# Uneven token parts (36 and 28 tiles instead of 32 and 32) and a later, denser routing of the first part

## The chip, the core and the metric

The kernel runs on one core of a Trainium2 chip, as one launch. The metric is the device time of that launch in microseconds (us). The engines are named as in the profile: PE (TensorE matmul), PEld (TensorE weight load), DVE (VectorE), ACT (ScalarE), POOL (GpSimd) and SP (SyncE, here a queue of DMA issues). Each engine runs its own instructions strictly in order and waits on semaphores.

## The reference

One transformer block on x of shape 4 x 2048 x 256 in f32 (8192 tokens, 64 tiles of 128 tokens). Six modulation vectors per batch come from `silu(c) @ wmod`; two of them gate the two branches.

```python
h = layernorm(x) * (1 + ca) + sa
x = x + ga * attention(h)            # 16 heads of 16, rotary, causal, exact softmax
h = layernorm(x) * (1 + cb) + sb
scores = sigmoid(h @ gate_w); sb_ = scores + gate_bias
# 4 groups of 4 experts: keep the 2 best groups (sum of their 2 best), then the 4 best experts
w = take(scores, tidx) / (sum + 1e-20) * 2.5
y = sum over the 4 chosen experts e of w_e * (silu(h @ w1[e].T) * (h @ w3[e].T)) @ w2[e].T
shared = (silu(h @ ws1.T) * (h @ ws3.T)) @ ws2.T
x = x + gb * (y + shared)
```

## The kernel before

A planner, `plan()`, writes one list of named items with all work in one order. Every engine walks this list and emits the instructions that are its own, so a place in the list is a place in the queue of each engine that has a part in the item.

**Front.** Layer norm, the q, k and v projections and the rotation of all tokens (to about 340 us).

**Attention.** 16 groups `g` (batch `g // 4`, four heads each) of 40 steps `i`. A step is a block of 128 keys against up to 512 queries for four heads: PE makes scores (`sa`, `sb`), ACT exponentiates two pairs (`exp`, L1650, 80 of them in a group), POOL zeroes the upper triangle of the diagonal blocks (`affine_select`, L1803; 16 of the 40 steps, among them the last four), and two steps later PE multiplies with V (`pv`, L1097). In the same steps PE and DVE find the row maxima of the next group (`max`, L1048 on PE, L1463 and L1466 on DVE, 160 per group, four a step; none in group 15).

**Pumps.** Other work is put between the steps by generators that are advanced at a given rate for each step with i >= 2 (`pumped`). `project(b)` is the output projection, the residual, the second layer norm and the router logits of the 16 tiles of batch b (seven items a tile; POOL does five instructions of it, L1816, L1819, L1827, L1833, L1835). Its first half runs from step 19 of group 3, 7, 11 and 15, its second in the next group; for batch 3 the second half lies in the expert stage. `route(p)` is the routing of token part p: a string of some 167 small DVE instructions (sigmoid, ranks by pairwise comparison, counts, slot numbers, L1231 to L1384), each waiting for the one before. `scatter(p)` follows: the slots' tail is zeroed by a DMA of 2 MB from SP (`zero`, L903, after a POOL memset L1839), 16 indirect DMAs for padding (`zpad`, L1844), and then for each tile a load of its rows into one of three buffers (`hs`, L911 on SP, which waits until the scatters of the tile three before have landed) and four indirect DMAs, one for each chosen expert (`scat`, L1852 on POOL).

**Experts.** Jobs of 128 slots, sorted by expert: 4 per tile and 15 of padding, so 143 for each part. Per job: a load of 128 rows (`jload`, L934 on SP), a transpose (`jin`, L1155 on PE), a copy (L1732 on ACT), twelve matmuls (`jgate`, L1170), silu on ACT (L1741), two products on DVE (L1578, L1579), the down projection (`jdown`, L1186) and a store. The load of a job of part p waits for every scatter of that part:

```python
for k in range(3):
    q.wait_ge(s[f"w_s{p}{k}"], s_last[p, k])
sync.dma_start(xq[n % XQ], xg_d[p][128 * i:128 * i + 128, :])
```

Jobs run part 0, then part 1, then 64 jobs of the shared expert. Beside part 0's jobs run the rest of `project(3)`, `route(1)` (5 items a job) and `scatter(1)` (2 a job). Beside part 1's jobs `collect(0)` sums the four expert outputs of each token of part 0: per tile four indirect gathers on POOL (`yg`, L1865), one scaling on ACT (L1701), three multiply-adds (`comb`, L1559), a gate (`gated`) and a residual (`res`) on DVE. Beside the shared jobs runs `collect(1)`; the output of a shared job (`fin`) adds that tile's sum, so the shared job of tile t of part 1 waits for `res` of that tile. At the border from part 1's jobs to the shared ones whatever is left of `collect(0)` is emptied into the list at once (`drain`).

In the attention stage before the change one generator holds both halves of the work, and what is left is emptied behind the last step:

```python
part0 = chain(route(0), scatter(0))
if g >= 8:
    pumps.append([part0, 0.0, 1.05 if g >= 12 else 1.4])
drain(part0)
```

Of the kernel before, what the change touches and what calls it, by code (L numbers as in the profile page):

```python
# [24 lines left out]
FIRST = (0, 32)  # L25
TILES = (32, 32)
# [11 lines left out]
ROUTE_SLOTS = 167  # L38
# [84 lines left out]
def plan():  # L123
# [185 lines left out]
    part0 = chain(route(0), scatter(0))  # L309
# [21 lines left out]
    for n, (g, i) in enumerate(order):  # L331
        if i == 0:
# [5 lines left out]
            if g >= 8:  # L338
                pumps.append([part0, 0.0, 1.05 if g >= 12 else 1.4])
# [43 lines left out]
    drain(part0)  # L383
# [45 lines left out]
    beside = {0: [[chain(proj[3], route(1)), 0.0, 5], [chain(once("route", 1, ROUTE_SLOTS - 1), scatter(1)), 0.0, 2.0]],  # L429
# [35 lines left out]
def program(nc, x, wqk, wv, bqk, bv, wo, ob, gw, gbias, w13, w2, cT, wmod, ropec, ropes, consts, fconst, out):  # L465
# [14 lines left out]
    with ExitStack() as ctx:  # L480
# [19 lines left out]
        tile_e = [tile_es[32 * p:32 * p + 1, :] for p in range(PARTS)]  # L500
# [10 lines left out]
        h2t = A("h2t", [128, 3, 256], F32)  # L511
# [240 lines left out]
        def t_h2(i):  # L752
            return s[f"w_h2{i % 3}"], rows_done["w_h2", i]
# [7 lines left out]
        def _(sync):  # L761
# [11 lines left out]
            for name, *at in o.items:  # L773
# [120 lines left out]
                elif name == "o_h2":  # L894
# [3 lines left out]
                    sync.dma_start(h2_d[128 * i:128 * i + 128, :], h2t[:, i % 3]).then_inc(s[f"w_h2{i % 3}"], 16)  # L898
# [64 lines left out]
        def _(pe):  # L963
# [16 lines left out]
            for name, *at in o.items:  # L980
# [132 lines left out]
                elif name == "o_turn":  # L1113
# [7 lines left out]
                    for f in (0, 1):  # L1121
                        mm = pe.transpose(PB[:, bank, 128 * f:128 * f + 128], h2t[:, i % 3, 128 * f:128 * f + 128], ident[:, :])
# [808 lines left out]
```

## Time and profile before

| | |
|---|---|
| median of 3 runs | 3035.09 us (3031.45 to 3038.47) |
| the profiled execution, its own time | 3028.71 us |
| its span in the trace | 3027.0 us |
| mean granted TensorE clock | 0.978 |
| PE, DVE, ACT, POOL busy | 92%, 76%, 59%, 41% |
| attention groups 1, 2, 5, 6 and 13 | 100.3 us each |
| first transpose of the expert stage, last transpose copy | 2104.28 us, 3006.16 us |

Times inside the trace count from the start of the span. "Busy" is an average over three stages with different limits; what a moved instruction costs has to be read in the group or job where it stands. A group is delimited below by the start of its first exponential (L1650) and that of the next group.

### The profile page before, as it was taken

The numbers are of one execution on the slowest core, as the hardware profiler recorded it, in microseconds if no ns is written. First come the engines' busy times: TensorE is split into PE (matmuls) and PEld (weight loads), VectorE is DVE, ScalarE is ACT, GpSimd is POOL, SyncE is SP. The second block draws the span as 40 slices with busy tenths as digits, with TensorE's granted clock in tenths as the row PEclk, the third lists the DMA queues.
The fourth block names the chain that finished last, engine by engine and source line by source line (L and its number), as shares of the span: only waits on it lengthen the run. The fifth ranks groups of instructions, "written<-read, shape, count | busy, mean of one in ns | idle before, by whom it ended". The sixth has DMA issues, their size and how long they took to land.

```text
span 3027.0 us, 57895 instructions
## 1 busy us (share of the span) xinstructions
PE 2796.0 (92%) x20452; PEld 1454.0 (48%) x20452; DVE 2295.2 (76%) x6063; ACT 1782.2 (59%) x2736; POOL 1252.7 (41%) x1557
## 2 busy tenths in 40 slices
PE   7888799999999999989998999988989999999997
PEld 4433222223332223322223322223888999999996
DVE  7888899998889999899998889932482225666477
ACT  2422476666566766656665567675566666666532
POOL 6766311213521114511113765555306744443276
PEclk9999899999999999999999999999999999999999
DMA  4853323223312332321323425245336756665486
GB/s 165 206 149 103 113 59 67 65 46 75 102 47 47 67 68 62 104 50 31 66 61 90 140 90 133 91 132 161 120 94 216 235 195 185 181 184 172 139 238 192
DMA packets 288762, 358.85 MB, mean 119 GB/s; under 512 B 63484, under 2 KB 241292, under 8 KB 288220
## 3 DMA queue, kind: packets, MB, share of 16 engines
q1 hardware_dynamic: 259740, 281.12, 34.0%
q0 software_dynamic: 26112, 71.34, 7.5%
q8 instruction: 166, 2.72, 0.4%
q10 hardware_dynamic: 2624, 2.69, 0.3%
q14 instruction: 120, 0.98, 0.1%
HBM read 206.25 MB, written 139.21 MB: 114 GB/s over the span
## 4 chain that ended last, share of the span: by engine, by line
PE 45%; DVE 16%; ACT 12%; POOL 7%; issue 7%; DMA 1%; ACTq 0%; SPq 0%; POOLq 0%; DVEq 0%
ACT P L1650 12%; PE PB L1170 11%; DVE mx L1466 7%; PE PB L1097 7%; PE PB L1186 7%; PE PB L1048 5%; PE PB L1067 5%; PE PB L1080 5%; DVE PB L1463 4%; POOL x_slots L1852 4%; PE PB L1155 2%; PE PB L1111 2%; POOL yg L1865 1%; PE PB L1134 1%; POOL x_slots L1844 1%
## 5 line engine op out<-in xcount | busy, mean ns | idle before, releaser
L1650 ACT ACTIVATE P<-PB 128x1024 f32<-128x1024 f32 (+3 forms) x1280 | 1097.6, 894 | 620.2 <-PE PB L1080 615.8
L1466 DVE TENSOR_REDUCE mx<-PB 128x1 f32<-128x512 f32 x1536 | 974.9, 683 | 110.2 <-PE PB L1048 103.3
L1048 PE MATMUL PB<-KO,QO 64*128 64x512 bf16 (+3 forms) x2560 | 769.9, 355 | 76.6 <-DVE mx L1466 36.7
L1097 PE MATMUL PB<-P,V 128*17 128x512 f32 (+3 forms) x5120 | 599.8, 541 | 10.5 <-POOL P L1803 10.4
L1067 PE MATMUL PB<-QO,KO 64*128 64x512 bf16 (+3 forms) x2560 | 543.6, 353 | 62.0 <-ACT P L1650 35.5
L1048 PEld LDWEIGHTS PB<-KO,QO 64*128 64x128 bf16 x2560 | 205.9, 94 | 778.0 <-DVE mx L1466 358.1
L1463 DVE CUSTOM_DVE_ANT_0 PB<-PB,mk 128x128 f32<-128x128 f32 (+3 forms) x1024 | 481.9, 510 | 35.5 <-PE PB L1048 33.2
L1080 PE MATMUL PB<-QO,KO 34*128 34x512 bf16 (+3 forms) x2560 | 502.8, 351 | 0.1
L1803 POOL TENSOR_SCALAR_AFFINE_SELECT P<-P 128x256 f32<-128x256 f32 x512 | 208.0, 412 | 656.9 <-ACT P L1650 651.4
L1170 PE MATMUL PB<-xT,ws 128*128 128x128 f32 x3432 | 433.7, 276 | 5.0 <-ACT xT L1732 5.0
L1170 PEld LDWEIGHTS PB<-xT,ws 128*128 128x128 f32 x3432 | 408.5, 193 | 6.8 <-ACT xT L1732 6.6
L1578 DVE TENSOR_TENSOR haT<-sl,PB 64x128 f32<-64x128 f32 x350 | 101.5, 290 | 401.2 <-ACT sl L1741 399.0
L1865 POOL DMA_INDIRECT yg<-y_slots,sidu x256 | 249.7, 976 | 301.5 <-DVE acc L1559 118.7
L1186 PE MATMUL PB<-W,haT 128*128 x1144 | 298.1, 383 | 11.2 <-DVE haT L1579 8.4
L1741 ACT ACTIVATE sl<-PB 128x256 f32<-128x256 f32 x350 | 134.2, 383 | 259.1 <-PE PB L1170 257.0
L1067 PEld LDWEIGHTS PB<-QO,KO 64*128 64x128 bf16 x2560 | 137.4, 94 | 254.7 <-ACT P L1650 224.2
L1725 ACT ACTIVATE ws<-W 128x768 f32 x286 | 239.4, 837 | 25.1 <-issue 25.1
L1080 PEld LDWEIGHTS PB<-QO,KO 34*128 34x128 bf16 x2560 | 164.5, 94 | 97.9 <-PE PB L1067 31.7
L1186 PEld LDWEIGHTS PB<-W,haT 128*128 128x128 f32 x1144 | 196.1, 191 | 30.3 <-issue 14.6
L1852 POOL DMA_INDIRECT x_slots<-Rsg,sidu x172 | 166.9, 970 | 84.2 <-ACT P L1650 47.4
L1810 POOL TENSOR_TENSOR osb<-osb,rden 128x512 f32<-128x512 f32 x64 | 82.3, 1286 | 242.1 <-DMA rden<-rden_rows 241.9
L1097 PEld LDWEIGHTS PB<-P,V 128*17 128x17 f32 x5120 | 85.3, 95 | 181.6 <-issue 152.8
(174 smaller groups left out, 3104.3 us busy)
## 6 DMA issues: line engine op xcount, KB each, us to landing
xq<-x_slots SPq DMA_DIRECT2D x286, 128.0 KB, 2.8
qk_parts<-pt SPq DMA_DIRECT2D x192, 128.0 KB, 2.4
KO<-qk_parts SPq DMA_DIRECT2D x192, 128.0 KB, 3.9
y_slots<-yo SPq DMA_DIRECT2D x191, 128.0 KB
QO<-qk_parts SPq DMA_DIRECT2D x64, 256.0 KB, 3.4
rden<-rden_rows SPq DMA_DIRECT2D x256, 64.0 KB, 2.1
y_slots<-mx SPq DMA_DIRECT2D x95, 128.0 KB
v_rows<-vst SPq DMA_DIRECT2D x16, 544.0 KB, 3.8
```

The lines of the kernel that those rows point to most:

```text
L1048: mm = pe.matmul(PB[:, bank, 0:n], QO[half, k3, j, 128 * t:128 * t + 128], KO[half, k3, j, 512 * kc:512 * kc + n], start=True, stop=True)
L1067: pe.matmul(PB[:, j, 0:n], KO[rows, k3, j, 128 * kt:128 * kt + 128], QO[rows, k3, j, q0:q0 + n], start=True, stop=False).then_inc(s["sa"], 1)
L1080: pe.matmul(PB[:, j, 0:n], KO[rows, k3, j, 128 * kt:128 * kt + 128], QO[rows, k3, j, q0:q0 + n], start=False, stop=True).then_inc(s["st"], 1)
L1097: mm = pe.matmul(PB[32 * j:32 * j + 17, 7, c0:512], V[:, g % 2, kt, 17 * j:17 * j + 17], P[:, pbuf(g, i, j // 2), j % 2, 0:n], start=kt == ...
L1170: mm = pe.matmul(PB[:, 2 + k, 128 * m:128 * m + 128], w[:, 128 * m:128 * m + 128], xT[:, k, f, :], start=f == 0, stop=f == 1)
L1186: mm = pe.matmul(PB[:, bank, 0:256], haT[:, k, f, :], w, start=f == 0, stop=f == 1)
L1463: dve.tensor_tensor_reduce(PB[:, u.bank[item], 0:n], PB[:, u.bank[item], 0:n], mk[:, 512 - n:512], 1.0, -3.0e38, ALU.add, ALU.max, mx[:, j ...
L1466: dve.tensor_reduce(mx[:, j, t, kc:kc + 1], PB[:, u.bank[item], 0:n], AX.X, ALU.max).then_inc(s["mx"], 1)
L1650: act.activation(P[:, pbuf(g, i, p), :, 0:n], PB[:, 2 * p:2 * p + 2, 0:n], ACT.Exp, scale=0.25).then_inc(s["exp"], 1)
L1725: act.activation(ws[:, k], W13[:, :, bass.ds(of[p, i], 1), :].rearrange("p f o c -> p f (o c)"), ACT.Copy).then_inc(s["ws"], 1)
L1852: pool.indirect_dma_start(xg_d[p][:, :], bass.IndirectOffsetOnAxis(sidu[:, i, j:j + 1], 0), hs[k], None).then_inc(s[f"w_s{p}{k}"], 16)
L1865: pool.indirect_dma_start(yg[:, k, j, :], None, y_d[p][:, :], bass.IndirectOffsetOnAxis(sidu[:, i, j:j + 1], 0)).then_inc(s[f"l_yg{k}"], 16)
```

## The change

Part 0 gets 36 tiles (tokens of batches 0 and 1 and the first four tiles of batch 2) and part 1 gets 28. So there are 159 and 127 jobs, 286 as before. The routing of part 0 needs the logits of four tiles of batch 2 and can't start before group 11. Routing and scatters become two generators: the routing takes 3.2 items a step from group 11 on, and the scatters 1.5 a step as soon as the routing is in the list. Routing tiles are [128, 36 x 16] and [128, 28 x 16]; counts over more than 32 tiles take two matmuls and two copies each. To make room, `h2t` has two buffers instead of three and the sums of tiles 32 to 35 lie in two buffers of the routing (`Rsb`, `Rcm`).

```diff
-FIRST = (0, 32)
-TILES = (32, 32)
+FIRST = (0, 36)
+TILES = (36, 28)
...
-ROUTE_SLOTS = 167
+HALVES = [[(t, min(t + 32, n)) for t in range(0, n, 32)] for n in TILES]
+ROUTE_SLOTS = [165 + 2 * len(x) + 2 * (n > 32) - 2 * (n <= 16) for x, n in zip(HALVES, TILES)]
...
-        while not o.has("o_logits", (FIRST[p] + TILES[p] - 1) // 16, 15):
+        while not o.has("o_logits", (FIRST[p] + TILES[p] - 1) // 16, (FIRST[p] + TILES[p] - 1) % 16):
...
-    part0 = chain(route(0), scatter(0))
+    def once(name, *at):
+        while not o.has(name, *at):
+            yield
+
+    routing = route(0)
+    scattering = chain(once("route", 0, ROUTE_SLOTS[0] - 1), scatter(0))
...
-            if g >= 8:
-                pumps.append([part0, 0.0, 1.05 if g >= 12 else 1.4])
+            if g >= 11:
+                pumps.append([routing, 0.0, 3.2])
+                pumps.append([scattering, 0.0, 1.5])
...
-    drain(part0)
+    drain(routing)
+    drain(scattering)
...
-    jobs += [("s", i // 32, i) for i in range(NT)]
+    jobs += [("s", int(i >= FIRST[1]), i) for i in range(NT)]
...
-        h2t = A("h2t", [128, 3, 256], F32)
+        h2t = A("h2t", [128, HT, 256], F32)
...
+        more = [r[:, :, :].rearrange("p t e -> p (t e)")[:, 256 * k:256 * k + 256] for r in (Rsb, Rcm) for k in (0, 1)]
+        acc = [*(acc_s[:, t, :] for t in range(ACC)), *more]
...
-                    if i >= 3:
-                        q.wait_ge(s["o_turn"], i - 2)
-                        q.wait_ge(*t_h2(i - 3))
+                    if i >= HT:
+                        q.wait_ge(s["o_turn"], i - HT + 1)
+                        q.wait_ge(*t_h2(i - HT))
```

By the list, the routing items of part 0 stood in groups 8 (16), 9 (53), 10 (53) and 11 (45); now 3 stand in the last step of group 11, 121 in group 12 and 47 in group 13. The 16 paddings and 128 scatters stood in groups 11 to 15 (7, 39, 39, 39 and 20), the last in step 21 of group 15; now the 16 paddings and 144 scatters stand in groups 13 (35), 14 (57) and 15 (68).

Three places. First DVE, in a step near the start of group 12, where the maxima of the next group (L1466, L1463; L1476, L1473 in the new file) and the projection of batch 2 stand. Before:

```order
L1508 TENSOR_TENSOR xo<-PB,obB 128x256
L1466 TENSOR_REDUCE mx<-PB 128x1 x4
L1537 COPY L<-PB 128x16
L1463 ISA PB,mx<-PB,mk 128x128
L1463 ISA mx 128x1
...
L1501 RECIPROCAL r_68<-d_67 128x16
L1466 TENSOR_REDUCE mx<-PB 128x1 x2
L1531 TENSOR_SCALAR h2t<-xin,mvf,rsf 128x256
L1514 BN_STATS st6f<-xin 128x6
```

Now, from the same tile's `xo` on:

```order
L1518 TENSOR_TENSOR xo<-PB,obB 128x256
L1258 MEMSET Rrk 128x576
L1239 TENSOR_TENSOR Rsa<-Rsa 128x36x3 x2
L1250 SCALAR_TENSOR_TENSOR Rsa<-Rsa 128x36x3
L1476 TENSOR_REDUCE mx<-PB 128x1 x2
L1511 RECIPROCAL r_68<-d_67 128x16
L1473 ISA PB,mx<-PB,mk 128x384
L1473 ISA mx 128x1
...
L1547 COPY L<-PB 128x16
L1239 TENSOR_TENSOR Rsa<-Rsa 128x36x2 x2
L1250 SCALAR_TENSOR_TENSOR Rsa<-Rsa 128x36x2
L1476 TENSOR_REDUCE mx<-PB 128x1 x4
```

Three or four routing instructions (`Rsa`, `Rrk`) now stand in each step among the maxima, on whose end PE's next maxima wait.

Second POOL, in the last steps of group 15. Before, there are the triangles of the last diagonal blocks (AFFINE_SELECT) and the projection of batch 3:

```order
L1810 TENSOR_TENSOR osb<-osb,rden 128x512
L1803 AFFINE_SELECT P<-P 128x2x128 x4
L1833 TENSOR_TENSOR h2t<-h2t,modB 128x256
L1835 TENSOR_TENSOR h2t<-h2t,modB 128x256
L1827 TENSOR_TENSOR rsf<-vef,mhalf 128x1
L1803 AFFINE_SELECT P<-P 128x2x128 x2
L1816 TENSOR_TENSOR xo<-xo,gaB 128x256
L1819 TENSOR_TENSOR xin<-xo,xin 128x256
```

Now:

```order
L1837 TENSOR_TENSOR rsf<-vef,mhalf 128x1
L1862 DMA x_slots<-Rrk,sidu 22528x256 x2
L1813 AFFINE_SELECT P<-P 128x2x128 x2
L1826 TENSOR_TENSOR xo<-xo,gaB 128x256
L1829 TENSOR_TENSOR xin<-xo,xin 128x256
L1862 DMA x_slots<-Rrk,sidu 22528x256
L1813 AFFINE_SELECT P<-P 128x2x128 x2
L1862 DMA x_slots<-Rrk,sidu 22528x256
L1862 DMA x_slots<-Rsg,sidu 22528x256 x8
L1862 DMA x_slots<-Rrk,sidu 22528x256 x4
```

One or two scatters (L1862) stand between the triangles of each step, and behind the last triangle stand 13 more, ahead of the first `jload` in the list.

Third DVE, at the border from the last job of part 1 to the first shared job. Before, only the job's own work stands there: the copy of part 1's output (L1587), the two products, and then the first sum with `acc` (L1590). `collect(0)` has ended twenty jobs earlier.

```order
L1587 COPY yo<-PB 128x256
L1578 TENSOR_TENSOR haT<-sl,PB 64x128
L1579 TENSOR_TENSOR haT<-sl,PB 128x128
L1590 TENSOR_TENSOR yo<-PB,acc 128x256
```

Now:

```order
L1597 COPY yo<-PB 128x256
L1588 TENSOR_TENSOR haT<-sl,PB 64x128
L1589 TENSOR_TENSOR haT<-sl,PB 128x128
L1569 SCALAR_TENSOR_TENSOR Rsb<-yg,wts,Rsb 128x256 x3
L1575 TENSOR_TENSOR Rsb<-Rsb,GB 128x256
L1581 TENSOR_TENSOR Rsb<-Rsb,xin 128x256
L1569 SCALAR_TENSOR_TENSOR Rcm<-yg,wts,Rcm 128x256 x3
L1575 TENSOR_TENSOR Rcm<-Rcm,GB 128x256
L1581 TENSOR_TENSOR Rcm<-Rcm,xin 128x256
...
L1600 TENSOR_TENSOR yo<-PB,acc 128x256
```

The last three tiles of `collect(0)` (33, 34 and 35; the last two with `Rcm`) stand there in one block of 15 DVE instructions, and the first gathers of `collect(1)` wait for its last multiply-add.

## Rows read from the trace of the kernel before

**Rows 1.** The page, part 1: busy us, share of the span, instructions

```profile
PE 2796.0 (92%) x20452; PEld 1454.0 (48%) x20452; DVE 2295.2 (76%) x6063; ACT 1782.2 (59%) x2736; POOL 1252.7 (41%) x1557
```

**Rows 2.** Windows by group: stretch, length, busy us of each engine, granted clock, DMA

```profile
446.85:547.15 100.30, 95.03 (x802) 26.62 (x802) 91.84 (x235) 69.78 (x84) 17.78 (x37) 1.00 0.26 55
...
759.09:880.89 121.80, 115.73 (x906) 41.73 (x907) 106.67 (x296) 75.00 (x97) 51.18 (x86) 0.99 0.28 76
...
1081.48:1193.12 111.64, 107.86 (x858) 35.60 (x858) 100.85 (x271) 72.02 (x88) 38.36 (x67) 1.00 0.33 76
1193.12:1320.81 127.69, 119.50 (x907) 42.88 (x907) 113.82 (x310) 75.52 (x98) 51.86 (x88) 0.96 0.27 72
1320.81:1431.09 110.28, 102.23 (x802) 29.39 (x802) 107.72 (x288) 69.90 (x84) 19.08 (x37) 0.98 0.23 50
1431.09:1540.46 109.37, 100.92 (x804) 28.34 (x805) 106.65 (x288) 69.90 (x84) 18.77 (x37) 1.00 0.23 50
1540.46:1667.03 126.57, 113.54 (x858) 37.27 (x858) 115.09 (x318) 72.04 (x88) 42.17 (x69) 0.97 0.34 89
1667.03:1796.72 129.69, 118.53 (x906) 42.22 (x907) 109.73 (x296) 75.06 (x97) 93.90 (x130) 0.96 0.41 120
1796.72:1897.02 100.30, 94.86 (x803) 26.58 (x803) 91.91 (x235) 69.74 (x86) 55.79 (x76) 1.00 0.45 119
```

**Rows 3.** Routing instructions on DVE by line: ns min/median/max, shapes

```profile
L1242 DVE SCALAR_TENSOR_TENSOR Rrk<-Rrk,Rcm x15: 211/415/648, 1357.9 to 1445.6; 128x480 f32<-128x480 f32 x1, 128x448 f32<-128x448 f32 x1, 128x416 f32<-128x416 f32 x1, 128x384 f32<-128x384 f32 x1
...
L1270 DVE RECIPROCAL Rsg<-Rrk x2: 3353/3353/3353, 1289.1 to 2182.2; 128x512 f32<-128x512 f32 x2
```

**Rows 4.** Timeline of POOL at the first padding: start, us, instruction, idle before

```profile
1657.15 1.23 POOL L1844 DMA_INDIRECT x_slots<-Rsa,zidu  x1 [7.20 <-DMA x_slots<-Rsa]
```

**Rows 5.** Scatters on POOL in group 13: ns min/median/max

```profile
L1852 POOL DMA_INDIRECT x_slots<-Rsg,sidu x27: 958/976/1008, 1797.4 to 1895.7; - x27
```

**Rows 6.** Windows, group 15 up to its last triangle

```profile
1996.64:2101.98 105.34, 91.64 (x692) 27.98 (x692) 11.55 (x40) 71.76 (x89) 58.83 (x89) 0.97 0.49 151
```

**Rows 7.** The chain that ended last, last padding of part 1: start, us

```profile
2303.71 2.77 DMA x_slots<-Rsa,zidu
```

**Rows 8.** Timeline of all engines where attention ends

```profile
2101.21 0.77 POOL L1803 TENSOR_SCALAR_AFFINE_SELECT P<-P 128x256 f32<-128x256 f32 x2
...
2102.19 1.33 SPq L934 DMA_DIRECT2D xq<-x_slots  x3
...
2104.28 0.69 PE L1155 MATMUL PB<-ident,xq 128*128 128x128 f32 x2 [1.75 <-DMA xq<-x_slots]
...
2109.62 0.44 PE L1155 MATMUL PB<-ident,xq 128*128 128x128 f32 x2 [2.52 <-DMA xq<-x_slots]
```

**Rows 9.** Windows of L1732, one per job: length, ACT busy (x jobs), clock, DMA

```profile
2107.60:2176.40 68.80, 7.63 (x20) 0.97 0.51 149
2176.40:2272.30 95.90, 12.57 (x33) 0.99 0.30 91
...
2855.30:2979.00 123.70, 19.54 (x51) 1.00 0.80 236
```

**Rows 10.** Timeline of the shared jobs: first and last gather of part 1, and the end

```profile
2855.25 0.94 POOL L1865 DMA_INDIRECT yg<-y_slots,sidu  x1 [73.80 <-DMA y_slots<-yo]
...
3006.16 0.36 ACT L1732 ACTIVATE xT<-PB 128x256 f32<-128x256 f32 x1
...
3015.14 1.22 PE L1186 MATMUL PB<-osb,haT 128*128 128x256 f32 x2 [4.05 <-DVE haT L1579]
...
3016.16 1.06 PE L1186 MATMUL PB<-rden,haT 128*128 128x256 f32 x2
...
3018.33 1.11 POOL L1865 DMA_INDIRECT yg<-y_slots,sidu  x1 [0.30 <-issue]
...
3021.78 1.53 DVE L1559 SCALAR_TENSOR_TENSOR acc<-yg,wts,acc 128x256 f32<-128x256 f32 x3 [2.14 <-ACT acc L1701]
...
3024.36 0.42 DVE L1590 TENSOR_TENSOR yo<-PB,acc 128x256 f32<-128x256 f32 x1
```

More of the change, by code:

```diff
@@ L257, in route @@
         o("route0", p)
-        while not o.has("o_logits", (FIRST[p] + TILES[p] - 1) // 16, 15):
+        while not o.has("o_logits", (FIRST[p] + TILES[p] - 1) // 16, (FIRST[p] + TILES[p] - 1) % 16):
             yield
         o("sge", p)
-        for k in range(ROUTE_SLOTS):
-            if k in (81, 82):
-                unit("cnt", p, k - 81)
+        for k in range(ROUTE_SLOTS[p]):
+            if 0 <= k - 81 < 2 * len(HALVES[p]):
+                unit("cnt", p, *divmod(k - 81, len(HALVES[p])))
             o("route", p, k)
@@ L428, in plan @@
             o("jload", n)
-    beside = {0: [[chain(proj[3], route(1)), 0.0, 5], [chain(once("route", 1, ROUTE_SLOTS - 1), scatter(1)), 0.0, 2.0]],
+    beside = {0: [[chain(proj[3], route(1)), 0.0, 5], [chain(once("route", 1, ROUTE_SLOTS[1] - 1), scatter(1)), 0.0, 2.0]],
               NI[0] - XQ: [],
@@ L499, in program @@
         tile_es = A("tile_es", [33, NI[0] + 1], I32)
-        tile_e = [tile_es[32 * p:32 * p + 1, :] for p in range(PARTS)]
+        tile_e = [tile_es[32 * p:32 * p + 1, 0:NI[p] + 1] for p in range(PARTS)]
         gw_s = A("gw_s", [128, 2, 16], F32)
@@ L752, in t_h2 @@
         def t_h2(i):
-            return s[f"w_h2{i % 3}"], rows_done["w_h2", i]
+            return s[f"w_h2{i % HT}"], rows_done["w_h2", i]
         packed = {n: (s[f"w_on{n % OS}"], 64 * (n // OS + 1)) for n in range(64)}
@@ L897, in _ @@
                     q.wait_ge(s["h2"], i + 1)
[L898 removed]
+                    sync.dma_start(h2_d[128 * i:128 * i + 128, :], h2t[:, i % HT]).then_inc(s[f"w_h2{i % HT}"], 16)
                 elif name == "zero":
@@ L1121, in _ @@
                     for f in (0, 1):
-                        mm = pe.transpose(PB[:, bank, 128 * f:128 * f + 128], h2t[:, i % 3, 128 * f:128 * f + 128], ident[:, :])
+                        mm = pe.transpose(PB[:, bank, 128 * f:128 * f + 128], h2t[:, i % HT, 128 * f:128 * f + 128], ident[:, :])
                     mm.then_inc(s["o_turn"], 1)
@@ L1313, in route @@
                 for m, dst in ((0, sa), (1, slot)):
-                    bank = u.bank["cnt", p, m]
-                    q.wait_ge(s["cnt"], o.n("cnt", p, m))
-                    prev()
-                    dve.tensor_copy(dst, PB[:, bank, 0:16 * PT].rearrange("p (t e) -> p t e", e=16)).then_inc(s["cnt_v"], 1)
-                    yield
-                q.wait_ge(s["cnt_v"], 2 * p + 2)
+                    for h, (lo, hi) in enumerate(HALVES[p]):
+                        bank = u.bank["cnt", p, m, h]
+                        q.wait_ge(s["cnt"], o.n("cnt", p, m, h))
+                        prev()
+                        dve.tensor_copy(dst[:, lo:hi, :],
+                                        PB[:, bank, 0:16 * (hi - lo)].rearrange("p (t e) -> p t e", e=16)).then_inc(s["cnt_v"], 1)
+                        yield
+                q.wait_ge(s["cnt_v"], 2 * sum(len(x) for x in HALVES[:p + 1]))
                 tt(slot, slot, sa, ALU.subtract)
```

39 lines of the change are left out of this document (19 added, 20 removed).

## The prediction

> **What bounds the kernel now.** The page gives PE 92% busy and DVE 76% [rows 1], but those are averages over stages, so I read the windows by group first. A plain attention group takes 100.30 us with DVE busy 91.84: DVE has 8.5 us of room. Groups with a projection take 111.64 (first half) and 121.80 (second half), with DVE at 100.85 and 106.67 [rows 2]. Groups 8 to 11 carry the routing of part 0, and the reader is to see two things in them [rows 2]: how much DVE's busy time grew over the like group without routing, and how much the group's length grew. Group 8: +7.15 busy, +5.9 length (over 121.80). Group 9: +15.9, +10.0 (over 100.30). Group 10: +14.8, +9.1. Group 11: +14.2, +14.9 (over 111.64). The routing is thus 52.1 us of DVE, and about two thirds of it shows as time: groups 9 and 10 leave DVE only 2.6 and 2.7 us idle, so there DVE is the bound, and PE waits for maxima. Group 11's surplus is larger than its neighbours' ratio would give. The timeline shows POOL stand still for 7.20 us in it, for the DMA that zeroes the slots' tail, with triangles queued behind it [rows 4]; I put 5.6 us of the 14.9 on that, 9.3 on routing. Group 12, with scatters and projection together, takes 129.69, 7.9 more than group 4 of the same make; group 13, with 39 scatters and no projection, takes exactly the plain 100.30 [rows 2]. So POOL's scatters cost nothing alone, and something beside a projection.
>
> Then the experts. Where nothing disturbs, 51 jobs take 123.70 us, 2.425 a job. The first 20 (beside the projection) take 3.44 each and the next 33 (beside the routing of part 1) 2.91 each [rows 9]. The end is not PE's: the last transpose copy is at 3006.16, yet the span ends at 3027.0. POOL issues 128 gathers from 2855.25 to 3018.33, one in 1.284 us without a pause, and the last sums and the last output hang on them [rows 10].
>
> **The change, term by term** (change of time in us, against the profiled execution's own 3028.71, which is 6.4 below the median 3035.09).
>
> *Routing leaves groups 8 to 11.* -5.9, -10.0, -9.1 and -14.9. In group 11's last step three instructions remain, with the reciprocal of 3.353 us, 576 instead of 512 elements now [rows 3]. In group 8 these and 13 small ones cost 5.9; I take 4.5. Sum -35.4.
>
> *Routing enters group 12.* A rank instruction goes from 0.211 us at 32 elements to 0.648 at 480 [rows 3], 0.98 ns an element, so an eighth more tiles makes the whole some 12% dearer: 52.1 becomes 58. About 5 of it is in group 11, 14 in group 13 (47 items, mostly on one partition), 39 in group 12. DVE there needs 106.67 + 39 = 145.7, and with the 2.6 us that groups 9 and 10 left idle the group can't be shorter than 148.3. PE's own work fills 115.73 of 121.80 in such a group, so the two will not fit together perfectly; bounds are 148.3 and 156, I take 151: +21 over 129.69. The scatter trouble of before's group 12 is gone from it, that is in the difference.
>
> *Group 13.* 14 us of routing in 15 steps, in which DVE has 8.5 x 15/40 = 3 us of room: +11. Zeroing and padding now fall here, in steps 16 to 27, with the diagonal steps 20 to 23 behind POOL's 7.20 us standstill: 2 to 7, I take 5. Together +16.
>
> *Group 14.* 57 scatters. One costs POOL 0.976 us [rows 5] and 0.30 of issue, 1.27. POOL had 55.79 busy with 39 of them [rows 2]; now 55.79 + 18 x 1.27 + 39 x 0.30 = 90 of 100. It fits, but a diagonal step of about 2.1 us gets 1.9 us of scatters and 0.8 of triangles: 0 to 6, I take 2.
>
> *Group 15 and the hand-over.* POOL was busy 58.83 of the 105.34 us up to its last triangle, with 21 scatters [rows 6] (the list has 20 in the group, one lags in from group 14). Of the 68 now, 55 stand ahead of that triangle: 58.83 + 34 x 1.27 + 21 x 0.30 = 108. POOL becomes the bound at the end of the group, above all in its second half, where the projection stands and steps need 2.9 us of POOL against 2.8; triangles, and so PE's `pv`, come late: 0 to 17, I take 8. Then come the 13 emptied scatters, 12 x 1.27 = 15 us to the last one's start, 2.77 until it has landed [rows 7], and the first job's load and transpose, 2.1 us after its issue [rows 8]; SP can't issue that load earlier, since it waits for all scatters. Before, PE began the first transpose 2.3 us behind the last triangle's end (2101.98 to 2104.28); now 20: +18. Some 3 come back, as PE's 2.52 us wait for the second load [rows 8] is hidden. Hand-over +15, together +23; bounds 15 and 32.
>
> *Experts.* The routing of part 1 has 28 tiles, some 10% less than before: 5 us of DVE, in 33 jobs that are 16 us above the floor; if two thirds show, as in attention, -3 (0 to -6). 16 fewer scatters, -1. Two buffers for `h2t` instead of three: the store of a tile is two of its successors old when the buffer is wanted again, 0.
>
> *The end.* Now 112 gathers. First what stands against it: `collect(0)` needs 224 pulls at 1.65 a job and has 127 jobs, so three tiles are emptied at the border, 3 x (1.53 for the multiply-adds + 2 x 0.42, an add of one tile) = 7.1 us of DVE at one place [rows 10]; PE is a job ahead, I take a stall of 5. The gathers of part 1 start some 5 us later, at 2860.2, and the last of 112 at 2860.2 + 111 x 1.284 = 3002.7. The end was 8.7 behind it (3018.33 to 3027.0), so gathers allow 3011.4. PE allows: last transpose copy at 2855.4 + 60 x 2.425 + 5 = 3005.9, products about one job's time later (2.4), down projection 2.1 (3015.14 to 3017.22) [rows 10], sum and store 2.64 (3024.36 to 3027.0), so 3013. The bound moves from POOL to PE: -14 (-19 without the stall, -9 if it is 10).
>
> Sum: -35.4 + 21 + 16 + 2 + 23 - 3 - 1 - 14 = **+8.6**, so 3037 for a profiled execution and 3044 for the median.
>
> **A rule weighed.** Scatters beside a full DVE take 0.958 to 1.008 us in group 13, where DVE is busy 91.91 of 100.30 [rows 2, 5]. The Trainium skill (SBUF — State Buffer, Who interferes with whom) says that while DVE runs an instruction in a mode that takes both ports, GpSimd can't write the descriptors of its DMAs, so that such a DMA looks blocked. The trace shows none of it, though maxima read PSUM, which may be why. It is the last rival below, with a price from rows.
>
> **The rivals.**
> 1. *No measurable change.* Each step on its cheap side: group 12 at 148.3 (-2.4), group 13 without a padding stall (-3), POOL not behind in group 15 (-8): 8.6 - 13.4 = -4.8, 3030. For it: scatters cost nothing in group 13. Against: POOL had waits for DVE in group 15 that are not in its busy time. Chance 0.20.
> 2. *Faster.* The late hand-over is given back. The first 53 jobs are (3.44 - 2.425) x 20 + (2.91 - 2.425) x 33 = 36 us above the floor, because PE waits for projection and routing; if POOL and DVE get ahead of PE while it waits for the first load, the 23 us return: 8.6 - 23 = -14, 3021. It decides from 15 us given back on. Against: the projection's PE work stands behind the first transpose in the list, so the chain can't run ahead. Chance 0.13.
> 3. *Clearly slower.* POOL falls behind from group 13 on, and each block of diagonal steps pays what before's standstill cost, 5.6 us; five such blocks in groups 13 to 15 are +28 less the 5 already counted: 3067. For it: the 2.7 us of POOL work in a diagonal step of 2.1. Chance 0.12.
> 4. *Scatters stretched by DVE.* If each of the 57 scatters of group 14 is held for one DVE instruction of about 0.65 us, POOL needs 90 + 37 = 127 us in a group of 100: +27, 3071. By the skill's page this is where it would show. The 0.976 us above speaks against it. Chance 0.05.
>
> **How the numbers follow.** The forecast has 0.50, its own range is 3032 to 3058 (the bounds of groups 12 to 15 and of the border stall, not all at one end). Eight in ten: from rival 2's 3021 to 3067, cutting rival 4 and the outer part of 2 and 3, so 3022 to 3066. A measurement of this kernel tells 0.2%, 6 us, from no change. Faster: rival 2 and a part of rival 1, 0.18. Same: the rest of rival 1 and the lower edge of the forecast, 0.25. Slower: 0.57.
>
> **What would show it.** In the changed profile: groups 8, 9 and 10 at 121.8, 100.3 and 100.3, and 11 at about 116; group 12 near 151 with DVE over 95% busy; group 13 near 116; POOL over 95% busy in the second half of group 15, and a gap of some 18 us on PE between the last `pv` and the first transpose, ended by the DMA of `xq`; jobs 20 to 52 at 2.8 us; a short stall of PE behind the last job of part 1; and an end 7 us behind the last transpose copy instead of 21. I would be wrong if group 12 came out far from 151, if the gap at the hand-over were under 10 or over 25 us, or if gathers still ended last.

## The result and the profile after

The changed kernel takes 3094.41 us (median of 4 runs, 3090.05 to 3104.14) against 3033.27 (3029.00 to 3038.47) for the kernel before beside it: ratio 1.0201, 95% interval 1.0183 to 1.0218. It is slower, as forecast, but by 61 us where I had 9, and outside the range. The profiled execution took 3104.14 us, its span is 3102.4. (Two of the four executions of the first experiment's kernel took 6596 and 10273 us; no execution of any other kernel did, the cause is unknown, and they are left out.)

The page and the windows by group (columns as in [rows 2]) answer to [rows 1] and [rows 2]:

```profile
PE 2841.1 (92%) x20453; PEld 1456.9 (47%) x20454; DVE 2302.1 (74%) x6051; ACT 1785.0 (58%) x2752; POOL 1252.3 (40%) x1557
```

```profile
1199.66:1321.91 122.25, 115.87 (x907) 41.54 (x907) 106.65 (x296) 75.00 (x97) 51.18 (x86) 0.99 0.28 75
1321.91:1422.21 100.30, 95.03 (x802) 26.61 (x803) 91.85 (x235) 69.78 (x85) 17.77 (x37) 1.00 0.26 55
...
1522.50:1634.85 112.35, 108.51 (x867) 35.83 (x867) 100.93 (x270) 72.62 (x90) 38.81 (x69) 1.00 0.32 77
1634.85:1819.50 184.65, 147.95 (x904) 47.42 (x901) 166.52 (x416) 75.58 (x97) 57.93 (x86) 0.81 0.18 50
1819.50:1948.77 129.27, 112.23 (x803) 29.68 (x803) 113.59 (x285) 69.91 (x85) 49.84 (x69) 0.85 0.36 97
1948.77:2048.59 99.82, 93.61 (x791) 26.02 (x791) 87.74 (x217) 69.58 (x85) 72.23 (x93) 1.00 0.37 117
2048.59:2194.99 146.40, 104.07 (x712) 30.70 (x713) 18.18 (x45) 73.31 (x92) 111.49 (x144) 0.79 0.57 183
```

The rows are groups 8, 9, 11, 12, 13, 14, and 15 with the hand-over (to the first transpose copy). The page hides the loss: DVE's total is only 7 us up. Group by group the two traces give:

| stretch | forecast | measured |
|---|---|---|
| groups 8 to 11 | -35.4 | -38.7 |
| group 12 | +21 | +55.0 |
| group 13 | +16 | +29.0 |
| group 14 | +2 | +0.2 |
| group 15 and hand-over | +23 | +35.4 |
| first transpose copy to that of job 286 | -4 | -1.2 |
| job 286 to the end | -14 | -10.7 |
| all ahead of group 8 | 0 | +6.5 |

The last line is the same program in both; its length differed by as much between other runs (the first exponential starts anywhere from 340.6 to 347.2 us). The stretches add up to +75.4 and not to the medians' +61.1: the profiled execution is the slowest of its four, and the one profiled before is faster than all four of its kernel. So some 14 us of the table belong to these two executions and not to the change.

In group 12 the waits name DVE: the projection's `h2t` and the maxima (engine, line and tile, what it waited for: us in total, times, longest; ahead of these stand only ACT's waits for PE's scores and POOL's for exponentials):

```profile
POOL h2t L1843 <- DVE h2t L1541: 39.9, 9, 9.4
PEld PB L1055 <- DVE mx L1473: 37.6, 29, 5.3
PEld PB L1055 <- DVE mx L1476: 24.5, 34, 3.9
...
PE PB L1055 <- DVE mx L1473: 22.5, 16, 4.8
```

Two pieces of the timeline of that group show what a routing instruction costs there, DVE first:

```profile
1659.88 0.31 DVE L1239 TENSOR_TENSOR Rsa<-Rsa 128x144 f32<-128x144 f32 x1
...
1664.03 0.73 DVE L1239 TENSOR_TENSOR Rsa<-Rsa 128x144 f32<-128x144 f32 x1
...
1668.46 0.58 DVE L1239 TENSOR_TENSOR Rsa<-Rsa 128x108 f32<-128x108 f32 x2
1669.08 0.27 DVE L1250 SCALAR_TENSOR_TENSOR Rsa<-Rsa 128x108 f32<-128x108 f32 x1
1669.26 1.28 DVE L1476 TENSOR_REDUCE mx<-PB 128x1 f32<-128x512 f32 x2
```

```profile
1663.79 0.81 POOL L1845 TENSOR_TENSOR h2t<-h2t,modB 128x256 f32<-128x256 f32 x1
```

First, in a row of three nothing overlaps: the third starts 0.62 us behind the first, whose pair took 0.58. But a maximum starts 0.18 us behind the last routing instruction, which takes 0.27. Over all 171 routing instructions ahead of the experts, one followed by another routing instruction, which waits for its result, held DVE for its own duration + 0.037 us on average, any other for its duration - 0.08. Second, the same instruction takes 0.31 us at 1659.88 and 0.73 at 1664.03, where POOL multiplies `h2t`. Against the same instructions in the expert stage of the kernel before (part 1's routing, scaled by 1.12 for the size), 27 of the first 81 were lengthened by more than 0.15 us, 10.9 us together, and each of the 27 overlapped with a TENSOR_TENSOR of POOL; in the kernel before 5 were, 1.4 us together. I call "hold" the time from the start of a routing instruction to the start of the next DVE instruction, summed over all: it is 63.3 us before (73 instructions stand alone and 94 in 47 pairs, so 47 are followed by another) and 90.3 after (rows of three and four, 117 followed by another).

At the hand-over the timeline answers to [rows 8]:

```profile
2171.67 0.77 POOL L1813 TENSOR_SCALAR_AFFINE_SELECT P<-P 128x256 f32<-128x256 f32 x2
...
2172.58 0.63 PE L1104 MATMUL PB<-P,V 128*17 128x128 f32 x8 [2.82 <-POOL P L1813]
...
2189.66 0.96 POOL L1862 DMA_INDIRECT x_slots<-Rrk,sidu  x1 [0.30 <-issue]
...
2192.14 1.27 SPq L941 DMA_DIRECT2D xq<-x_slots  x3
...
2194.26 0.69 PE L1163 MATMUL PB<-ident,xq 128*128 128x128 f32 x2 [21.05 <-DMA xq<-x_slots]
```

PE stands still for 21.05 us, with 13 scatters between the last triangle and the load. Of these 13 only one had to wait, the one at 2185.87 (2.13 us, for the rows of its tile). A scatter takes what it took in [rows 5], here in group 14:

```profile
L1862 POOL DMA_INDIRECT x_slots<-Rsg,sidu x38: 954/960/1011, 1948.2 to 2048.7; - x38
```

And the end, against [rows 10]: last gather, last transpose copy, last sum.

```profile
3090.06 0.94 POOL L1875 DMA_INDIRECT yg<-y_slots,sidu  x1 [0.30 <-issue]
...
3093.82 0.38 ACT L1742 ACTIVATE xT<-PB 128x256 f32<-128x256 f32 x1 [0.23 <-PE PB L1163]
...
3099.27 0.94 DVE L1600 TENSOR_TENSOR yo<-PB,acc 128x256 f32<-128x256 f32 x2
```

The span ends 8.6 us behind the last transpose copy, where it was 20.8. Gathers no longer end last.

### The profile page after: what moved, and what is told of

Its sections match the earlier page's. It is cut to its first block, busy times and chain, and to the rows that moved or that the text cites. A ratio compares the mean times of both kernels' runs of the same rounds, so it can differ in the third digit from the quotient of the medians.

```text
span 3102.4 us, 57909 instructions
## 1 busy us (share of the span) xinstructions
PE 2841.1 (92%) x20453; PEld 1456.9 (47%) x20454; DVE 2302.1 (74%) x6051; ACT 1785.0 (58%) x2752; POOL 1252.3 (40%) x1557
## 4 chain that ended last, share of the span: by engine, by line
PE 48%; DVE 14%; ACT 13%; issue 6%; POOL 5%; DMA 2%; ACTq 0%; SPq 0%; DVEq 0%; POOLq 0%
ACT P L1660 13%; PE PB L1178 12%; PE PB L1194 8%; PE PB L1104 7%; PE PB L1074 6%; PE PB L1055 6%; DVE mx L1476 5%; PE PB L1087 5%; POOL x_slots L1862 3%; DVE PB L1473 3%; PE PB L1163 2%; PE PB L1118 2%; PE PB L1141 1%; POOL x_slots L1854 1%; DVE Rcm L1239 1%
## 5 line engine op out<-in xcount | busy, mean ns | idle before, releaser
L1476 DVE TENSOR_REDUCE mx<-PB 128x1 f32<-128x512 f32 x1536 | 974.8, 683 | 131.1 <-PE PB L1055 124.2
L1055 PE MATMUL PB<-KO,QO 64*128 64x512 bf16 (+3 forms) x2560 | 778.6, 361 | 94.9 <-DVE mx L1473 40.9
L1104 PE MATMUL PB<-P,V 128*17 128x512 f32 (+3 forms) x5120 | 613.4, 552 | 20.9 <-POOL P L1813 20.8
L1074 PE MATMUL PB<-QO,KO 64*128 64x512 bf16 (+3 forms) x2560 | 555.8, 362 | 61.5 <-ACT P L1660 33.8
L1473 DVE CUSTOM_DVE_ANT_0 PB<-PB,mk 128x128 f32<-128x128 f32 (+3 forms) x1024 | 481.9, 511 | 43.8 <-PE PB L1055 40.7
L1087 PE MATMUL PB<-QO,KO 34*128 34x512 bf16 (+3 forms) x2560 | 513.8, 359 | 0.1
L1862 POOL DMA_INDIRECT x_slots<-Rsg,sidu x172 | 166.0, 965 | 60.6 <-issue 42.5
```

What stands on the lines that cost most here:

```text
L1055: mm = pe.matmul(PB[:, bank, 0:n], QO[half, k3, j, 128 * t:128 * t + 128], KO[half, k3, j, 512 * kc:512 * kc + n], start=True, stop=True)
L1074: pe.matmul(PB[:, j, 0:n], KO[rows, k3, j, 128 * kt:128 * kt + 128], QO[rows, k3, j, q0:q0 + n], start=True, stop=False).then_inc(s["sa"], 1)
L1087: pe.matmul(PB[:, j, 0:n], KO[rows, k3, j, 128 * kt:128 * kt + 128], QO[rows, k3, j, q0:q0 + n], start=False, stop=True).then_inc(s["st"], 1)
L1104: mm = pe.matmul(PB[32 * j:32 * j + 17, 7, c0:512], V[:, g % 2, kt, 17 * j:17 * j + 17], P[:, pbuf(g, i, j // 2), j % 2, 0:n], start=kt == ...
L1473: dve.tensor_tensor_reduce(PB[:, u.bank[item], 0:n], PB[:, u.bank[item], 0:n], mk[:, 512 - n:512], 1.0, -3.0e38, ALU.add, ALU.max, mx[:, j ...
L1476: dve.tensor_reduce(mx[:, j, t, kc:kc + 1], PB[:, u.bank[item], 0:n], AX.X, ALU.max).then_inc(s["mx"], 1)
```

## The experiments

Each was run beside the kernel before (its median 3034.5 to 3035.6 us). Windows have the columns of [rows 2]. A profile is of one execution; where a time stands without a ratio, it is that of one execution.

**Routing one at a time.** The same 36 and 28 tiles and the same number of routing instructions a step, but drawn at four places of it, between the maxima:

```diff
-                pumps.append([routing, 0.0, 3.2])
+                spread = [[routing, 0.0, 0.8]]
```

> The changed kernel with the same 3.2 routing items a step, but put one at a time at four places between the maxima of the step instead of three or four in a row. Group 12 took 184.7 us in the changed kernel against 129.7 before. Theory A (rows of dependent routing instructions on DVE: each pays its whole latency, start to next start 0.52 us against 0.34 before, and PE stands for the length of the row, so its granted clock falls): group 12 falls to 150 to 162 us with a granted clock over 0.93, group 13 to 115 to 122, the total to 3055 to 3070. Theory B (VectorE simply has too much work in these groups, wherever it stands): group 12 stays at 175 to 185, the total at 3085 to 3100.

`spread` is advanced at four places of each step. Profiled execution 3061.53 us, another 3063.23, some 0.9% over before. Groups 12, 13, and 15 with the hand-over:

```profile
1628.06:1784.08 156.02, 132.12 (x904) 45.73 (x902) 149.05 (x413) 75.31 (x98) 57.71 (x86) 0.92 0.23 59
1784.08:1909.88 125.80, 110.70 (x802) 29.08 (x803) 111.39 (x287) 70.12 (x85) 49.27 (x68) 0.88 0.37 99
...
2009.75:2155.05 145.30, 98.78 (x712) 30.49 (x713) 17.35 (x45) 73.36 (x91) 112.82 (x145) 0.83 0.57 185
```

Group 12 falls from 184.65 to 156.02 and DVE's busy time in it by 17.5 us, with the same instructions. The hold falls from 90.3 to 70.2 us, and 6 instructions are lengthened (2.5 us). In group 12, 6 of them are followed by another where 83 were: 77 times the 0.12 us between the two cases makes 9 us, and the lengthening that is gone 8.4, together DVE's 17.5. In the timeline a routing instruction of 0.21 us is followed by a maximum 0.12 us after its start:

```profile
1665.02 0.21 DVE L1246 TENSOR_TENSOR Rsa<-Rsa 128x36 f32<-128x36 f32 x1
1665.14 0.68 DVE L1483 TENSOR_REDUCE mx<-PB 128x1 f32<-128x512 f32 x1
```

So 28.6 of group 12's 55 us go with how the instructions stand. Of these, 17.5 are DVE's work; the other 11 are no larger than what equal groups can differ by (see the scatters' rate below). Group 13 is only 3.5 us shorter, over what was expected of it.

**Routing without a projection beside it.** Routing starts in group 13 (3.2 a step in one row), scatters follow at 3 a step.

```diff
-            if g >= 11:
+            if g >= 13:
                 pumps.append([routing, 0.0, 3.2])
-                pumps.append([scattering, 0.0, 1.5])
+                pumps.append([scattering, 0.0, 3.0])
```

> The changed kernel with the routing two groups later, in groups 13 and 14, where no projection runs beside it; scatters at 3 a step behind it. Only groups 12 and 13 are to be compared: group 13 now has 121 routing items in rows of three and no projection. Theory B2 (it is the projection beside it that makes group 12 dear: its GpSimd instructions hold VectorE's two-input instructions up, 0.4 us each): the surplus of group 13 over a plain group is under 40 us (140 us or less) against 63 us over group 4's 121.8 in the changed kernel. Theory A (the rows themselves): the surplus stays over 50 us (150 us or more). Group 12, with neither routing nor scatters, takes 122 us by both.

3136.56 us. Groups 12 and 13:

```profile
1626.63:1747.26 120.63, 114.32 (x906) 41.22 (x907) 106.49 (x296) 74.95 (x97) 51.19 (x86) 1.00 0.30 77
1747.26:1895.85 148.59, 119.19 (x805) 32.10 (x807) 141.86 (x353) 70.69 (x86) 19.13 (x39) 0.86 0.17 37
```

The surplus over a plain group is 48.3 us, between the two theories' numbers, for 50.0 more of DVE, against 62.9 over a like group in the changed kernel's group 12, for 59.8. Only 8 instructions are lengthened (3.1 us). So the rows cost most of it without the projection, and POOL's multiplications of the projection some 8 us of DVE on top, by the count of lengthened instructions. DVE idles 6.7 us here and 18.1 in group 12 of the changed kernel. I read this as the projection, whose items go from PE to DVE to POOL and back, being held up by the rows too; no run separates it. The rest of the longer total stands in groups 14 and 15 (161.9 us, and 172.1 with the hand-over), where the scatters run at 3 a step; what they cost there wasn't looked into.

**More work for PE.** In groups 12 and 13 the first score matmul of each block is issued twice.

```diff
+                    if g in (12, 13):
+                        pe.matmul(PB[:, j, 0:n], KO[rows, k3, j, 128 * kt:128 * kt + 128], QO[rows, k3, j, q0:q0 + n],
+                                  start=True, stop=True)
```

> The changed kernel with every first score matmul of groups 12 and 13 done twice (the first result is overwritten): 320 more matmuls, about 32 us more TensorE work a group at full clock. Theory C (the fall of the granted clock to 0.81 and 0.85 in groups 12 and 13, after TensorE has stood for VectorE, is itself a large part of the loss): with TensorE kept busy the granted clock stays over 0.95 and group 12 takes no longer than 185 us, perhaps 170, in spite of more work. Rival (the clock is a by-product, VectorE sets the time): group 12 takes 185 to 190 at a higher clock. If TensorE's work adds up instead, group 12 takes 200 or more.

3102.11 us, group 12:

```profile
1632.99:1821.06 188.07, 152.07 (x1065) 53.95 (x1062) 167.20 (x416) 75.17 (x98) 57.16 (x85) 0.88 0.18 49
```

161 more matmuls lengthen the group by 3.4 us, while the granted clock rises from 0.81 to 0.88. PE had room for them. The idea that PE's lowered clock is what makes group 12 long finds no support: the clock rose and the group got longer. It isn't excluded as a part of the loss, since 0.88 stays short of the 0.95 that the test was to reach, and the matmuls that raise it are work of their own; see also the scatters' rate below.

**Even halves with the new schedule.** 32 and 32 tiles, all else as changed.

```diff
-FIRST = (0, 36)
-TILES = (36, 28)
+FIRST = (0, 32)
+TILES = (32, 32)
```

> The changed kernel with the old split of 32 and 32 tiles, all else as changed: the routing of part 0 falls into groups 11 (121 items) and 12 (46), the scatters end in group 14. This separates the schedule from the split. By the measured groups: group 11 pays what group 12 paid, 111.6 + 55 = 165 to 170; group 12 121.8 + 30 = 152; the hand-over of attention to experts as before (group 15 with hand-over 108 to 111 us, not 146); end of the kernel gather-bound as before, 20 us behind the last transpose copy. Total 3070 to 3085. If the split itself is what costs, the total is within 10 us of before.

3073.41 us, ratio 1.0123 (1.0090 to 1.0157). Routing falls in groups 11 and 12, and no scatter is left behind group 15. Groups 11, 12, and 15 with the hand-over:

```profile
1513.49:1676.90 163.41, 134.10 (x864) 40.19 (x869) 150.91 (x389) 72.83 (x89) 40.87 (x69) 0.86 0.23 53
1676.90:1831.79 154.89, 131.84 (x906) 43.79 (x906) 129.31 (x344) 75.74 (x97) 84.98 (x118) 0.88 0.35 104
...
2032.16:2142.20 110.04, 94.65 (x708) 29.78 (x708) 16.27 (x46) 73.01 (x92) 39.34 (x69) 0.95 0.41 128
```

The new schedule (with the two buffers of `h2t`, which belong to it here) thus loses 1.2%; the split itself adds 0.8: in the traces 36 us at the hand-over (146.40 against 110.04) and 9 in groups 8 to 13, less the 10.7 that the end gives back. The smaller `h2t` wasn't tried alone; in group 8, with the projection and without routing, it shows nothing (122.25 us, against 121.80 for the like group before).

**No scatters behind the group.** On top of the first experiment, 1.75 scatters a step.

```diff
-                pumps.append([scattering, 0.0, 1.5])
+                pumps.append([scattering, 0.0, 1.75])
```

> Compared with the spread schedule (e1_spread, profiled run 3061.53 us), only the rate of scatters goes from 1.5 to 1.75 a step, so that the list holds none behind the last exponential of group 15 instead of 14. There the last scatter decides when expert work can start: group 15 with hand-over took 145.30 us. Theory H (the emptied scatters are serial time behind the group, about 1.27 us each): hand-over falls by 13 x 1.27 = 16, so group 15 with hand-over about 129 and the kernel about 3045. Rival P (POOL's total work from the end of the routing on is what bounds, 111 us busy in group 15): the scatters only move from behind the group into it, diagonal steps get longer, group 15 with hand-over 138 to 145, or group 14 grows over 100, and the kernel is at 3055 to 3062.

3057.94 us. Groups 12, 14, and 15 with the hand-over:

```profile
1629.81:1794.62 164.81, 143.58 (x905) 48.03 (x901) 149.06 (x413) 75.30 (x97) 57.42 (x86) 0.84 0.21 55
...
1919.05:2023.04 103.99, 93.05 (x791) 26.36 (x791) 88.02 (x217) 69.81 (x84) 81.37 (x103) 1.00 0.39 126
2023.04:2148.23 125.19, 101.92 (x718) 31.01 (x718) 17.42 (x44) 73.09 (x91) 97.05 (x130) 0.88 0.59 189
```

From the last exponential to the first transpose copy it is 6.6 us instead of 26.3, group 15 itself stays at 118.6, and group 14 pays 4.1. The emptied scatters are serial time, as theory H says (19.8 us less, where it had 16). The total doesn't show it, since group 12, unchanged, came out 8.8 us longer than in the first experiment, DVE equally busy (149.06 and 149.05), PE at clock 0.84 instead of 0.92 and busy 11 us longer. So equal work in such a full group can differ by 9 us, and the longer one had the lower clock; which of the two is the cause isn't shown.

**Nothing emptied at the border.** On top of the first experiment, `collect(0)` at 1.85 a job.

```diff
-              NI[0] + 3: [[chain(shared_down(), collect(0)), 0.0, 1.65]],
+              NI[0] + 3: [[chain(shared_down(), collect(0)), 0.0, 1.85]],
```

> Compared with e1_spread, collect(0) runs at 1.85 pulls a job instead of 1.65, so that nothing of it is emptied at the border from part 1's jobs to the shared ones. Theory of the border: the 15 DVE instructions emptied there cost the changed kernel 6 to 7 us (jobs 286 to 300 took that much longer than before); they vanish, the stretch from the copy of job 286 to that of job 300 falls by 6 to 7, and gathers of part 1 can start earlier. The kernel 5 to 7 us below e1_spread. Rival: the time comes back in jobs 160 to 286, which carry the same work closer together, by 0.01 to 0.05 us a job, or at the end, where PE or the gathers set the last output: then 0 to -2.

3049.98 us. The copies of jobs 286 to 300 (columns: ACT busy, clock, DMA) take in the changed kernel

```profile
2934.26:2974.78 40.52, 5.35 (x15) 0.92 0.65 189
```

and here

```profile
2886.93:2920.87 33.94, 5.38 (x14) 1.00 0.68 195
```

as in the kernel before:

```profile
2848.17:2882.10 33.93, 5.36 (x14) 1.00 0.67 198
```

The stall of 6.6 us (5.8 in the first experiment) is gone and nothing comes back in the jobs ahead (the 128 jobs from 158 to 286 take 310.2 us here, 310.1 there). From job 286 to the end it is 161.3 us instead of the first experiment's 169.3, 8 us less.

**The projection out of group 15.** On top of the first experiment, the first half of the last projection runs beside expert jobs.

```diff
-            if g % 4 == 3:
+            if g % 4 == 3 and g < 15:
```

> Compared with e1_spread, the first half of the last projection (batch 3) leaves group 15 and runs beside the first expert jobs like its second half. 14 scatters still stand behind the last exponential. Theory H: POOL loses 5 instructions a tile for 8 tiles (about 20 to 25 us of its 111 us) in group 15, so that the triangles are no longer late there: group 15 from 118 to about 105, hand-over behind it unchanged at about 27, together about 131 instead of 145; jobs 0 to 60 get 8 to 14 us longer, since 8 tiles of projection move there: the kernel 3055 to 3062. Rival P (POOL's scatters alone set the length, 68 at 1.27 = 86 us plus triangles 26): group 15 with hand-over 140 or more and the kernel slower than e1_spread, about 3070.

3052.31 us, group 15 with the hand-over:

```profile
2005.64:2132.61 126.97, 83.19 (x655) 20.96 (x656) 4.97 (x6) 71.23 (x87) 88.11 (x110) 0.86 0.58 187
```

Up to the last exponential it takes 101.8 us instead of 119.0, the hand-over behind it stays at 25.1, and jobs 0 to 60 take 14.3 us longer. POOL's lag in group 15 needs both, scatters and projection. Of the 18.3 us that group and hand-over save, the jobs take 14.3 back, so that only some 4 of the 9 us by which this execution is shorter than the first experiment's are the edit's.

**The kernel before with its routing spread.** Only the place in the step changes: four places at a quarter of the rate, from group 8 on. Padding and scatters come from the same generator and are spread with the routing.

```diff
-                pumps.append([part0, 0.0, 1.05 if g >= 12 else 1.4])
+                spread = [[part0, 0.0, (1.05 if g >= 12 else 1.4) / 4]]
```

> The kernel before (32 and 32 tiles, its own start in group 8 and its own rates) with one change: the generator of routing and scatters is advanced at four places of a step at a quarter of the rate instead of once. Theory A (a routing instruction that stands alone between two maxima overlaps with them, several in a row pay their whole latency): the kernel before has 91 routing instructions that stand alone and 38 pairs; all of the pairs would stand alone, 38 x 2 x about 0.07 us, so 3 to 6 us less in groups 8 to 11, groups 9 and 10 at 107 to 109 instead of 110.3 and 109.4, ratio 0.998 to 1.000. Rival (a routing instruction holds back a maximum wherever it stands): no change, ratio 1.000. Slower over 0.2% would speak against both: then scatters or zeroing at another place of the step delay triangles in groups 12 to 15.

3023.07 us (5 runs, 3019.40 to 3028.32), ratio 0.9961 (0.9947 to 0.9975): faster than both kernels, and by more than I expected. Groups 8 to 10:

```profile
1193.42:1317.46 124.04, 115.71 (x906) 42.52 (x907) 112.53 (x309) 75.52 (x97) 51.72 (x88) 1.00 0.27 74
1317.46:1424.43 106.97, 100.14 (x803) 29.32 (x803) 105.57 (x288) 69.91 (x85) 18.84 (x37) 1.00 0.23 52
1424.43:1531.44 107.01, 100.09 (x804) 27.45 (x804) 103.80 (x288) 69.89 (x84) 19.45 (x37) 1.00 0.24 51
```

Every routing instruction stands alone (the kernel before has 73 alone and 47 pairs in its trace, not the 91 and 38 that I had), the hold falls from 63.3 to 55.2 us, and groups 8 to 11 are 9.8 us shorter. Four of them are followed by an instruction that reads SBUF and doesn't wait for them; it starts 0.07 us before their end, as the maxima do. So the overlap is lost where the next instruction waits for the result, and not because it reads SBUF.

**The kernel before with its routing in rows.** The mirror image: as many in each group, but three in a row at every third advance.

```diff
+    def bunched():
+        while True:
+            bunch[0] += 1
+            if bunch[0] % 3 == 0:
+                for _ in range(3):
+                    next(part0, None)
+            yield
...
-                pumps.append([part0, 0.0, 1.05 if g >= 12 else 1.4])
+                pumps.append([part0 if g >= 12 else bunched(), 0.0, 1.05 if g >= 12 else 1.4])
```

> The kernel before (32 and 32 tiles, routing from group 8 on, the same number of routing instructions in each group) with one change: in groups 8 to 11 the generator gives three instructions in a row at every third advance instead of one at each. Theory A (in a row each instruction pays its whole latency and the maxima behind it wait; an item followed by another routing item occupied DVE its duration + 0.037 us, one followed by a maximum its duration - 0.11): some 73 more items are followed by another, 11 us, up to 20 with what POOL holds up; groups 9 and 10 at 113 to 117 instead of 110.3 and 109.4, groups 8 to 11 together 12 to 25 us longer, total 3045 to 3057, ratio 1.004 to 1.008. Rival (what costs is the routing's share of DVE in a group, not how it stands): groups 9 and 10 within 1 us of 110, ratio 1.000 to 1.001. Second rival (rows leave whole steps free, in which PE and DVE catch up): faster than before.

3059.91 us, ratio 1.0073 (1.0048 to 1.0099). Groups 8 to 10:

```profile
1194.11:1324.15 130.04, 118.42 (x907) 42.60 (x907) 114.48 (x311) 75.57 (x98) 52.04 (x88) 0.97 0.26 71
1324.15:1439.20 115.05, 103.46 (x803) 30.08 (x803) 111.34 (x286) 69.81 (x85) 18.51 (x37) 0.96 0.21 48
1439.20:1556.63 117.43, 103.18 (x803) 29.39 (x805) 110.45 (x289) 70.01 (x84) 19.08 (x37) 0.96 0.23 47
```

The hold rises from 63.3 to 74.5 us (111 instructions followed by another, 47 before: 64 more and not 73), with only two instructions lengthened (1.1 us), and groups 8 to 11 grow by 22.1. Both rivals fall. Of these 22 us DVE's busy time has 12.1, of which the hold is 11.2; for the other 10 DVE stood idle. Group 12, where nothing was changed, is 6.1 us longer too, at a clock of 0.92 against 0.96, so that not all of the idle time need be the rows'.

**The three repairs together**, 36 and 28 tiles: four places, 1.75 scatters, 1.85 at the border.

> 36 and 28 tiles with the three repairs together: routing at four places of a step, scatters at 1.75 a step (none behind the last exponential), collect(0) at 1.85 a job (nothing emptied at the border). If the three costs are separate, the gains add: from e1_spread's 3061.5 about 12 for the hand-over (16 to 20 less there, 4 more in group 14) and 8 for the border, so 3040 to 3046, ratio to before 1.002 to 1.004. What is left over before is then group 12 (+26), group 13 (+24), group 15 (+15) against groups 8 to 11 (-39) and the end. Rival (one cause passes its time to the next): 3050 or more.

3045.39 us (6 runs, 3037.34 to 3051.38), ratio 1.0030 (1.0010 to 1.0050), as the sum of the parts said. Groups 12 to 15 still take 69.7 us more than before's, against 40.4 saved in groups 8 to 11 and 17.5 from job 286 on.

## Why the prediction was wrong

**The failed step: "Routing enters group 12".** It priced the routing at 39 us of DVE and put the group at DVE + 5. Measured are 59.8 and DVE + 18.1. The price came from the growth of DVE in groups 8 to 11 [rows 2], where 120 of 167 routing instructions were followed by a maximum and overlapped with it. I carried it to rows of three and four, which I had even written down as the new order. Standing alone they would have cost nearly that: 42.4 us of DVE and 156.0 in the first experiment, at the edge of my 148.3 to 156. The remaining 28.6 us went when the rows were taken away, and rows added to the kernel before cost time there too. Of these, 17.5 are DVE's busy time and shown: 9 for the lost overlap and 8.4 (10.9 less 2.5) for instructions lengthened beside POOL. The other 11 are idle time of DVE, and how much of it is the rows' stays open: another kernel with single instructions, whose group 12 took 164.8 us with DVE as busy, leaves only 19.8 of the 28.6. That DVE would be over 95% busy in this group was wrong as well: it was 90%, since the idle time grew with the work.

The Trainium skill (Perfetto Trace Analysis, Optimizing Scalar/DVE Operations) says that the write-acknowledgement half of a DVE instruction's profiled latency overlaps with the next instruction. The traces agree for a maximum behind a routing instruction (-0.07 to -0.14 us in the kernel before, -0.08 in the median) and show the limit of it: behind an instruction that the next one waits for it isn't there (+0.034 in the median). The Trainium skill (SBUF — State Buffer, Who interferes with whom) also says that a DVE instruction with two inputs in SBUF contends with a GpSimd instruction that reads SBUF. That agrees with the 0.31 and 0.73 us above. I had weighed that section only for the other direction, scatters held up by DVE; that rival is refuted by the 0.960 us of group 14.

**"Group 13"** had +16. The padding's standstill was right (step 22 takes 7.7 us instead of 1.9: +5.8 for my 5). The routing ahead of it costs 23 for my 11, the same mis-sized term: 21.7 us of DVE instead of 14. But here the rows are not the main cause: spreading them brought back only 3.5 us, 2.2 of them DVE's (3.5 to 5.6 over the kernels that do it). Part of it is what stands there: besides 34 instructions on one partition 15 of full size (0.75 us each), three more than in the like group 11 before. What makes up the rest, with DVE busy 111 of 126 us once they are spread, stays open.

**"Group 15 and the hand-over"** had the mechanism and sized it low: 15.6 in the group for my 8 (bound 17), 19.8 behind it for my 15. The lag appears behind the diagonal steps of all four blocks (4.4, 7.2, 11.6 and 15.6 us against the kernel before), not in the second half alone. Two experiments confirm the two parts one at a time.

**Groups 8 to 11, group 14** and **the end** were right: -38.7, +0.2 and a PE-bound end 8.6 us behind the last transpose copy, for my 7, though the end gained 10.7 for my 14. The border stall is 6.6 for my 5, and the next experts gave back 1.2 of the 4 that I had. None of the rivals came as it stood. Nothing of the late hand-over was given back. Rival 3's mechanism came in one group: in group 15 each of the four blocks of diagonal steps paid (4.4, 2.8, 4.4 and 4.0 us), in group 14 none did, and POOL stood still in group 13 once.

## What to carry to other kernels

A price read from a trace holds for the neighbours that the instruction had there: before using it at another density, look whether it still stands between independent work, or behind one that it waits for. Thin work that fills another stage's gaps should be drawn one instruction at a time at several places of a step; here that alone made the kernel before 0.4% faster, and rows of three made it 0.7% slower. What is emptied behind a stage was serial time here: a rate that leaves nothing took 19.8 us off the hand-over and cost 4.1 in the group before.

## What was not expected of the hardware

The same TENSOR_TENSOR of 144 elements takes 0.31 us or 0.73 us on DVE, the longer one while POOL runs a two-input multiplication. And with the same instructions in the same order, a full group took 156.0, 156.2, 156.1 and 156.1 us at a granted clock of 0.92 in four kernels and 164.8 at 0.84 in a fifth, so that a single profile of such a group is good to 9 us only. The first experiment's and the fifth kernel's rows stand above; these are the other three (no emptying at the border, no projection in group 15, the three repairs):

```profile
1628.41:1784.57 156.16, 132.60 (x905) 45.41 (x902) 148.95 (x413) 75.29 (x97) 57.29 (x86) 0.92 0.22 59
1626.06:1782.12 156.06, 132.40 (x905) 45.45 (x902) 148.74 (x413) 75.28 (x97) 57.36 (x86) 0.92 0.22 59
1626.79:1782.86 156.07, 132.19 (x905) 45.70 (x902) 149.11 (x413) 75.29 (x98) 57.73 (x86) 0.92 0.22 59
```
